# The first attention item's maxima inside the last tiles of the first sparse layer, and that layer's last tile shared by two engines

## The reference, cut to what matters

```python
x = x + lru_block(layernorm(x))       # linear recurrence, MLP, layernorm
x = x + sparse_layer(layernorm(x))    # "ffn(0)" below
x = x + attention(layernorm(x))       # 8 heads of 64, keys and values from a latent of 64
x = x + sparse_layer(layernorm(x))    # "ffn(1)" below
```

```python
score_out = softmax(gated_bottleneck_out(z)); score_in = softmax(gated_bottleneck_in(z))
out_branch = where(score_out in its top 32, (z @ weight) * score_out, 0)
in_branch  = where(score_in  in its top 32, z * score_in, 0) @ weight
return out_branch + in_branch + bias
```

## Time and profile before

| | |
|---|---|
| median of 3 runs | 1378.83 us (1377.39 to 1380.7) |
| profiled execution, its own time | 1377.57 us |
| its span (first to last instruction) | 1375.6 us |
| first sparse layer, its 32 tiles | about 290 to 500 us |
| attention, starts of its first and last exponential | 502.98 and 1131.6 us |
| PE, DVE, ACT, POOL busy | 89, 83, 77, 70% of the span |

### The profile page before, as it was taken

The page is one execution under the profiler, slowest core; times in us unless marked ns, Lnnn a source line. Parts: engine busy times, 40 slices in busy tenths (PEclk is TensorE's granted clock), DMA queues, the critical chain, the costliest instruction groups (busy, mean ns, idle before and its releaser), DMA issues.

```text
span 1375.6 us, 30660 instructions
## 1 busy us (share of the span) xinstructions
PE 1219.7 (89%) x10192; PEld 745.8 (54%) x10192; DVE 1145.5 (83%) x3141; ACT 1054.7 (77%) x2351; POOL 962.1 (70%) x1100
## 2 busy tenths in 40 slices
PE   3999999867888879999999999999999999677776
PEld 1455555434455536665666666666666667344443
DVE  6999998589998888888777787877878754799998
ACT  3332333677899869999999989999999995787776
POOL 4456644368777777778777778777777773388887
PEclk9899999989999999999999999999999999799998
DMA  6200000000012000010000000000000000000000
GB/s 174 77 1 1 0 0 1 1 1 1 10 38 78 27 21 25 25 26 25 25 14 14 2 2 2 2 3 2 2 2 2 2 3 1 1 31 16 25 22 32
DMA packets 35529, 25.32 MB, mean 18 GB/s; under 512 B 16358, under 2 KB 32044, under 8 KB 35372
## 3 DMA queue, kind: packets, MB, share of 16 engines
q1 hardware_dynamic: 35372, 23.36, 6.0%
HBM read 14.89 MB, written 8.39 MB: 17 GB/s over the span
## 4 chain that ended last, share of the span: by engine, by line
PE 58%; ACT 13%; issue 12%; DVE 11%; POOL 4%; DVEq 0%; DMA 0%; SPq 0%; POOLq 0%; ACTq 0%
PE banks L2023 7%; PE banks L2025 6%; PE banks L2011 6%; DVE arena L1535 4%; PE banks L1761 4%; PE banks L1969 4%; PE banks L1720 4%; PE banks L2040 4%; PE banks L2041 4%; PE banks L2042 3%; ACT arena L1174 3%; DVE arena L1530 3%; ACT arena L1182 2%; PE banks L1748 2%; PE banks L1776 2%
## 5 line engine op out<-in xcount | busy, mean ns | idle before, releaser
L839 POOL TENSOR_TENSOR arena<-arena 128x512 f16<-128x512 f32 x383 | 437.6, 1161 | 150.5 <-ACT arena L1182 146.6
L1174 ACT ACTIVATE arena<-banks 128x512 f32<-128x512 f32 x512 | 302.9, 599 | 45.5 <-PE banks L2025 40.8
L1611 DVE TENSOR_REDUCE arena<-banks 128x1 f32<-128x512 f32 x512 | 325.8, 680 | 4.0 <-PE banks L2011 1.8
L1182 ACT ACTIVATE arena<-arena 128x512 f16<-128x512 f32 x512 | 316.2, 632 | 0.0
L1530 DVE MAX8 arena<-arena 128x8 f32<-128x256 f32 x512 | 190.4, 414 | 27.4 <-issue 15.9
L2040 PE MATMUL banks<-arena 128*128 128x65 f16 x2016 | 211.4, 193 | 0.9
L2041 PE MATMUL banks<-arena 128*128 128x64 f16 x2016 | 211.5, 195 | 0.0
L2042 PE MATMUL banks<-arena 128*128 128x65 f16 x2016 | 210.6, 193 | 0.0
L1637 DVE TENSOR_TENSOR arena<-arena 128x512 f16<-128x512 f32 x129 | 107.0, 829 | 123.2 <-ACT arena L1182 123.0
L1535 DVE MATCH_REPLACE8 arena<-arena 128x256 f32<-128x256 f32 x512 | 206.2, 411 | 0.9 <-issue 0.2
L2040 PEld LDWEIGHTS banks<-arena 128*128 128x128 f16 x2016 | 187.9, 96 | 31.8 <-issue 9.9
(11 more groups left out here) (229 smaller groups left out, 2545.1 us busy)
## 6 DMA issues: line engine op xcount, KB each, us to landing
arena<-q_store SPq DMA_DIRECT2D x48, 128.0 KB, 2.7
x<-in_L_attn_a_x SPq DMA_DIRECT2D x8, 512.0 KB, 3.9
q_store<-arena SPq DMA_DIRECT2D x32, 128.0 KB, 1.8
out<-x SPq DMA_DIRECT2D x7, 512.0 KB, 2.9
arena<-arena SPq DMA_DIRECT2D x64, 1.0 KB, 1.9
arena<-in_L_attn_a_W_in SPq DMA_DIRECT2D x1, 768.0 KB, 5.8
arena<-in_L_attn_a_W_mid SPq DMA_DIRECT2D x1, 512.0 KB, 7.6
arena<-in_L_attn_a_w_w SPq DMA_DIRECT2D x2, 256.0 KB, 8.0
```

Of the source, the lines that this page charges most:

```text
L839: nc.gpsimd.tensor_tensor(pr_lo[c][:, kt, :], pr[:, kt, :], pr_hi[c][:, kt, :], ALU.subtract).then_inc(a_lP, 1)
L1174: nc.scalar.activation(pr[:, kt, :], ps[6 + kt % 2][:, :], ACT.Exp, scale=SM_SCALE).then_inc(a_P, 1)
L1182: nc.scalar.activation(pr_hi[c][:, kt, :], pr[:, kt, :], ACT.Copy).then_inc(a_hi, 1)
L1611: nc.vector.tensor_reduce(mx_half[c][:, i // 2, i % 2:i % 2 + 1], ps[n % MAX_BANKS][:, :], X, ALU.max).then_inc(a_mx, 1)
```

## The change

It consists of these parts:

1. The eight maxima of item 0 are made inside `ffn(0)`: PE makes one at the end of `head_first(t)` of t = 22, 23, 25, 26, 27, 28 and two at t = 29, in banks 2 and 3; DVE reduces them between the second and the third round of tile t+2, and adds `largest(0)` in tile 31. ACT's `max_scaled(0)` comes before its `ffn_gs` of tile 30.
2. `scores(0, 0)` stands on PE between `ffn_full(31)` and `ffn_in(31)`, and `exps(0, 0)` on ACT between `ffn_fs` and `ffn_gs` of tile 31. The in-branch of tile 31 goes to bank 3 instead of 6.
3. The last tile is shared: DVE (`first_tail`) makes the in-branch's difference and product and x plus bias, POOL (`tail_shared`) the other four steps. Waits for the end of the layer stand now at single places in items 0 and 1.
4. The maxima of item 1 are made during item 0, and of the later items with a lead that grows from item to item, by a table (`max_until`): after the steps of item 0, 10, 12, 14, 16, 17, 17, 18 and 19 maxima have been made, counted with the eight of item 0. In items 1 to 5 step 7 has two instead of one. From item 5's end on the lead is two items, as before.
5. `max_scaled(W+1)` stands at kt = 5, 6, 5, 4 in items 0 to 3 and at kt = 3 from item 4 on (`max_row_at`).

```diff
+        HEAD_MAX_AT = {22: (0,), 23: (1,), 25: (2,), 26: (3,), 27: (4,), 28: (5,), 29: (6, 7)}
+        HEAD_MAX_BANK = (2, 3, 2, 2, 3, 3, 2, 3)
+        LEAD = 6
+        def max_until(W, kt):
+            if W == 0:
+                return HALVES + (2, 4, 6, 8, 9, 9, 10, 11)[kt]
+            ahead = min(W + 2, HALVES) + kt + 1 + (1 if kt == KT - 1 and W < LEAD else 0)
+            return min((W + 1) * HALVES + ahead, ALL * HALVES)
+        def max_row_at(W):
+            return max(3, min(KT - 1, 2 + min(kt for kt in range(KT) if max_until(W, kt) >= (W + 2) * HALVES)))
...
+            def tail_shared(t, p):
+                T = t
+                pool.wait_ge(f_e, T * 2 + 2)
+                pool.wait_ge(f_er, T * 2 + 2 + CREDIT["f_er"])
+                nc.gpsimd.tensor_tensor(dd[p][:, 0, :], ex[p][:, 0, :], exr[p][:, 0, :],
+                                        ALU.subtract).then_inc(f_d, 2)
...
+            tail_shared(NT - 1, 1)
+            pool.wait_ge(f_x, NT + CREDIT["f_x"])
...
                 ffn_fs(f, NT - 2, 0)
+                if f == 0:
+                    max_scaled(0)
                 ffn_gs(f, NT - 2, 0)
                 ffn_rest(f, NT - 1, 1)
...
                 ffn_fs(f, NT - 1, 1)
+                act.wait_ge(f_s, NT)
+                exps(0, 0)
                 ffn_gs(f, NT - 1, 1)
...
-            max_scaled(0)
-            act.wait_ge(f_x, NT + CREDIT["f_x"])
...
-                    if kt == 3 and W + 1 < ALL:
+                    if W + 1 < ALL and kt == max_row_at(W):
                         max_scaled(W + 1)
...
                     topk_first(f, t, t % 2)
                     if t:
                         over_sums(f, t - 1, (t - 1) % 2)
+                    if f == 0:
+                        for i in HEAD_MAX_AT.get(t - 2, ()):
+                            largest_of(0, i)
+                            if i == HALVES - 1:
+                                largest(0)
                     topk_rest(f, t, t % 2)
...
+            def first_tail(t, p):
+                T = t
+                dve.wait_ge(f_x, T - 1 + CREDIT["f_x"])
+                dve.wait_ge(f_er, T * 2 + 1 + CREDIT["f_er"])
+                nc.vector.tensor_tensor(dd[p][:, 1, :], ex[p][:, 1, :], exr[p][:, 1, :],
+                                        ALU.subtract).then_inc(f_d_last, 1)
+                dve.wait_ge(f_d_last, 1)
+                dve.wait_ge(f_z, T + 1)
+                dve.wait_ge(f_s, T)
+                nc.vector.tensor_tensor(sx[p], dd[p][:, 1, :], zf[t % Z_RING], ALU.mult).then_inc(f_s, 1)
+                dve.wait_ge(f_xb, T)
+                nc.vector.tensor_tensor(xb[p], x[:, t, :], fbias[:, :], ALU.add).then_inc(f_xb, 1)
             ffn(0)
-            for W in range(2):
-                for i in range(HALVES):
-                    largest_of(W, i)
-                largest(W)
+            first_tail(NT - 1, 1)
...
-                    if W + 2 < ALL:
-                        largest_of(W + 2, kt)
+                    for n in range(max_from(W, kt), max_until(W, kt)):
+                        largest_of(n // HALVES, n % HALVES)
+                        if n % HALVES == HALVES - 1:
+                            largest(n // HALVES)
+                    if (W, kt) == (0, 0):
+                        dve.wait_ge(f_gs, NT + CREDIT["f_gs"])
+                    if (W, kt) == (0, 4):
+                        dve.wait_ge(f_x, NT + CREDIT["f_x"])
                     if kt in (LAST_DVE if W == ALL - 1 else LOW_DVE):
                         low(W, kt)
...
+                for i in HEAD_MAX_AT.get(t, ()):
+                    pe.wait_ge(*head_read[HEAD_MAX_BANK[i]])
+                    max_scores(0, i)
+                    head_read[HEAD_MAX_BANK[i]] = (a_mx, i + 1)
...
                 if t == NT - 1:
-                    pe.wait_ge(f_lg, NT)
-                    for i in range(2):
-                        max_scores(0, i)
-                    pe.wait_ge(*head_read[2])
-                    for i in range(2, HALVES):
-                        max_scores(0, i)
+                    pe.wait_ge(f_gs, NT - 1 + CREDIT["f_gs"])
+                    scores(0, 0)
             ffn(0)
-            for i in range(HALVES):
-                max_scores(1, i)
...
                 for kt in range(KT):
-                    scores(W, kt)
-                    if W + 2 < ALL:
-                        max_scores(W + 2, kt)
+                    if W or kt:
+                        scores(W, kt)
+                    for n in range(max_from(W, kt), max_until(W, kt)):
+                        max_scores(n // HALVES, n % HALVES)
                     if kt in WEIGHTED_AT and W:
                         weighted(W - 1, WEIGHTED_AT[kt])
```

More of the change, by code:

```diff
@@ L434, in over_chunks, with in_bank @@
                 step(n, n % 2, behind=n > 0, ahead1=n + 1 < NCH, ahead2=n + 2 < NCH, ahead4=n + 4 < NCH)
+        def in_bank(f, t):
+            return 3 if f == 0 and t == NT - 1 else 6
         def xc_bank(f, n):
@@ L782, in tail @@
                                         ALU.add).then_inc(f_x, 1)
+            def tail_shared(t, p):
[4 more added lines that the diff above has]
+                                        ALU.subtract).then_inc(f_d, 2)
+                pool.wait_ge(f_d, T * 2 + 2)
+                pool.wait_ge(f_fs, T + 1 + CREDIT["f_fs"])
+                nc.gpsimd.tensor_tensor(ob[p], fs[p], dd[p][:, 0, :], ALU.mult).then_inc(f_ob, 1)
+                pool.wait_ge(f_ob, T + 1)
+                pool.wait_ge(f_xb, T + 1)
+                nc.gpsimd.tensor_tensor(obx[p], ob[p], xb[p], ALU.add).then_inc(f_obx, 1)
+                pool.wait_ge(f_obx, T + 1)
+                pool.wait_ge(f_gs, T + 1 + CREDIT["f_gs"])
+                pool.sem_inc(s_turn, 1)
+                nc.gpsimd.tensor_tensor(x[:, bass.ds(t, 1), :], gs[p].unsqueeze(1), obx[p].unsqueeze(1),
+                                        ALU.add).then_inc(f_x, 1)
             def tail_last(f, t, p):
@@ L822, in ffn @@
                     pool.wait_ge(s_prep, 4 + CLEARED)
-                for t in range(NT - f):
+                for t in range(NT - 1):
                     tail(f, t, t % 2)
@@ L1049, in ffn_gs @@
                 act.wait_ge(f_gps, T + 1)
-                nc.scalar.activation(gs[p], ps[6][:, 0:D], ACT.Copy, scale=rinv[p][:, 1:2]).then_inc(f_gs, 1)
+                nc.scalar.activation(gs[p], ps[in_bank(f, t)][:, 0:D], ACT.Copy, scale=rinv[p][:, 1:2]).then_inc(f_gs, 1)
             def ffn_fs(f, t, p):
@@ L1227, in _ @@
                 for kt in range(KT):
-                    exps(W, kt)
+                    if W or kt:
+                        exps(W, kt)
                     if kt:
@@ L1610, in largest_of @@
                     wait_from(dve, a_mw, W - 1)
-                nc.vector.tensor_reduce(mx_half[c][:, i // 2, i % 2:i % 2 + 1], ps[n % MAX_BANKS][:, :], X,
+                bank = n % MAX_BANKS if W else HEAD_MAX_BANK[i]
+                nc.vector.tensor_reduce(mx_half[c][:, i // 2, i % 2:i % 2 + 1], ps[bank][:, :], X,
                                         ALU.max).then_inc(a_mx, 1)
@@ L1891, in ffn_in @@
                 for k in range(KB2):
-                    last = mm(ps[6][:, 0:D], sxT[p][:, k, :], fW[:, k, :], start=k == 0, stop=k == KB2 - 1)
+                    last = mm(ps[in_bank(f, t)][:, 0:D], sxT[p][:, k, :], fW[:, k, :], start=k == 0, stop=k == KB2 - 1)
                 last.then_inc(f_gps, 1)
@@ L2008, in max_scores @@
                     pe.wait_ge(a_dup, query_done(W))
-                wait_from(pe, a_mx, n - MAX_BANKS + 1)
+                if n < HALVES:
+                    wait_from(pe, a_mx, max([0] + [m + 1 for m in range(n) if HEAD_MAX_BANK[m] == HEAD_MAX_BANK[n]]))
+                elif n == HALVES:
+                    pe.wait_ge(a_mx, HALVES)
+                else:
+                    pe.wait_ge(a_mx, n - MAX_BANKS + 1)
+                bank = n % MAX_BANKS if W else HEAD_MAX_BANK[i]
                 every = qA[:, slot, c * CH:c * CH + CH].rearrange("p (q j) -> p j q", j=TPC)
-                mm(ps[n % MAX_BANKS][:, :], every[:, j, :], kA[B % 2][:, half * CH:half * CH + CH],
+                mm(ps[bank][:, :], every[:, j, :], kA[B % 2][:, half * CH:half * CH + CH],
                    start=True, stop=True).then_inc(a_mps, 1)
```

16 lines of the change are left out of this document (10 added, 6 removed).

## The result

The changed kernel takes 1381.02 us (median of 20 executions, 1378.39 to 1384.81). The kernel before, run beside it, takes 1377.55 us (20 executions, 1375.1 to 1380.7). The ratio is 1.0022, with a 95% interval of 1.0014 to 1.0031: 3.0 us slower, where I had predicted 1.5 us slower and called it no difference. The interval lies above 1, so the small difference shows over that many executions.

The account below looks back on a forecast made before the run. Two tight loops (DVE/ACT/PE in tiles, PE/ACT in items) with a slack 10.9 us join between; 3.65 - 1.75 - 1.4 - 2.0 = -1.5, so 1.5 us slower, 1380.3 us predicted; own range 1378.3 to 1382.2, 8 in 10 1375.7 to 1383.3.

Parts of the forecast that it names:

- Step 1: Late tiles: six maxima on PE, behind which ACT waits, make the loop 1.3 us later; bounds 0 and 1.3.
- Step 2: Tile 31: two maxima and the item's maximum on DVE move the last reciprocal 1.4 us later.
- Step 3: Join: shared last tile and early exps(0, 0) let exps(0, 1) start at 499.85 instead of 503.5, gaining 3.65 us.
- Step 4: Item 0: making item 1's maxima inside it, paced by DVE, loses 1.75 us of the gain; 1.9 left.
- Step 5: Items 1 and 2: rows of maxima arrive later by DMA, costing 1.3 us in item 1 and 0.2 in item 2.
- Step 6: Step 7 of items 2 to 5: second maximum makes PE wait for DVE, 0.5 us each, 2.0 in all; bounds 0 and 0.7.
- rival 2: Ramp, items 1 to 5: 0.7 us lost each in step 7, plus 0.3 more each; 1383.3 us; chance 0.14.

Follow-up runs that it names:

- e4_ahead_of_query: Changed kernel, with PE making item 0's six maxima in the tiles ahead of the next query instead of behind it; 1380.64 us in one run.
- e3_busy: Changed kernel plus 8 and 6 unread PE matmuls ahead of the in-branches of tiles 30 and 31; 1379.52 us, median of 12, ratio 1.0011 to the kernel before.
- e2_lead5: Changed kernel with the lead ending at 5 maxima, extra maxima only in items 0 to 2, max_scaled at kt 4 from item 3; 1379.65 us in one run.
- e1_step4: Changed kernel, with the second maximum of items 1 to 5 made in step 4 instead of step 7; 1383.48 us in one run.
- e8_const_busy: Changed kernel with constant lead of 5 maxima, item 0's maxima ahead of the query, 8 and 4 unread matmuls; 1369.49 us, ratio 0.9940 to the kernel before.

## Why the prediction was right or wrong

The sign and the range held: 1.5 us slower predicted, 3.0 (1.9 to 4.3) measured. The mechanism held in all steps but the third, whose time I had at the wrong clock.

- **Step 1** (six maxima in the tiles, 1.3): 1.20 measured, and `e4_ahead_of_query` shows that the reason was right.
- **Step 2** (1.4): 1.44.
- **Step 3** failed in its size. The last reciprocal to `exps(0, 1)` was to take 5.05 us and took 6.71. In the two traces with the clock held it took 4.62, so the chain as I had it was 0.4 too long, nearly all of it in the shared tile (1.77 us for 2.13). The missing 2.1 us are the clock. I had taken PE's durations from the earlier trace rows, at 2.4 GHz, for a stretch in which the engine had 1.2. On the shared tile I had weighed a rule of the Trainium skill (SBUF — State Buffer, "Who interferes with whom"): a VectorE operation with two SBUF inputs contends with a GpSimd one that reads SBUF. The first of the pair can't show it: it took 0.42 us (0.46 in the earlier trace rows), and POOL stood idle beside it until 492.46. The second, which starts together with POOL's, took 0.43 (0.83 there). The third, x plus bias, began at 492.80 while POOL's ran on to 493.47, and took 0.95 on as many elements. That agrees with the rule, and costs nothing in this chain, as PE waits for the second.
- **Step 4** (item 0 loses 1.75): from exps(0, 1) to exps(0, 5) 5.66 us, as forecast 5.75. The gain left at the first `weighted` is 0.38 instead of 1.9. In `e3_busy` it is 2.5. The difference between the two is all of step 3.
- **Step 5** (row late, 1.3 in item 1 and 0.2 in item 2): item 1 lost 1.03. Item 2 lost 1.08, where steps 5 and 6 had 0.5 in all: 0.64 by what they describe, as in `e3_busy`, and 0.44 by the row of item 3, which landed after 2.8 us. I had taken the median of the earlier trace rows, 1.9, for every row; its maximum, 2.8, stands beside it.
- **Step 6** (0.5 each in items 2 to 5): the mechanism is as I had it, and `e2_lead5` removes it with the second maximum. The price was 0.65, near my upper bound of 0.7; moving the second maximum to another step (`e1_step4`) saved only 0.1 of it. Of rival 2's mechanism that is the part that came true; its further 0.3 in every item did not.

With the clock held at the join and the row in time the sum closes. In `e3_busy` item 1 begins 2.2 us earlier than before the change (t24 + 70.83 against 73.03), items 1 to 6 lose 3.4 (1.03, 0.64, three times 0.64, less 0.15), and exps(7, 0) starts 1.2 us later. My -1.5 was near for that kernel. That its times say 1.5 us too is partly luck: its interval goes from 0.3 to 2.9, and both its traces hold the fall in item 33, worth some 1.4 to 1.7 us, which the one trace of before has not. The 3.0 us of the changed kernel, likewise, are measured; how they divide over many executions between the join's falls, slow rows and falls elsewhere is not. What I left out is that a change which moves PE's work ahead of and behind a pause can have the clock fall just there. The trace of before had the pause (0.32 and 0.66 of 2 us) and no fall, and I took that for safe. Why it did not fall there no run shows. Of the nine traces here with the new join and no unread matmuls eight show a fall there, of 3.4 to 10.2 us; the three with unread matmuls show none.

## What to carry to other kernels

Before moving work of TensorE across a stretch in which it is nearly idle, price the work behind it at both clock levels, and profile more than one execution: a fall may come in one and not in the next, and the place moves. A lead that grows item by item is paid in each item in which it grows; set it up once, where engines are free, and let it be as small as the slowest consumer (here the row's DMA, 1.9 us as a rule and up to 3.4) asks for. An operation in a tight loop costs by its place in the engine's order: the same six matmuls cost 1.2 us behind the query and 0.1 ahead of it.

## What the runs showed of the hardware

The granted clock falls to half (1.2 GHz) for a while after stretches in which TensorE was busy little (in the eight traces that fell, 0.06 to 0.65 of some 2 us not long before), and the clock of the same program with the same pause fell in one execution and not in the next. The kernel before had such a stretch too (0.32 of 2 us) and no fall there in its trace. At that level four matmuls of 256 columns took 2.07 us instead of 1.13, though they came in a stretch in which TensorE was busy most of the time (6.55 of 8 us). The Trainium skill (TensorE: Matmul & The Clock Gate, "HAM oscillation — how this bites in real kernels") tells of such falls after idle gaps in a loop and advises an order of work in which the engine stays busy; `e3_busy` agrees with the advice.

The same 1 KB DMA from SBUF to SBUF landed 1.9 us after its issue in the median, and after 2.6 to 3.4 us now and then (2.8 in the changed kernel, 3.1 in `e4_ahead_of_query`, 3.4 in `e8_const_busy`); a pipeline that allows for the median alone then waits 0.3 to 0.5 us.
